# Moving group moments, similarity scaling and a skip connection from VectorE to ScalarE and TensorE in a 16-image Mamba block

## What is computed

```
x = x + L0(gn(x))       # nearest dictionary word of each pixel by cosine similarity;
                        # where (1 - sim)/2 < 0.625 the pixel becomes that word (256 words)
x = x + L1(gn(x))       # layer norm over channels; 4 chunks of 64 channels, each through a Mamba
                        # block (in_proj, causal conv, silu, selective scan with 16 states,
                        # gate by silu(z), out_proj), + skip_scale * chunk; layer norm; proj
```

## Time and profile before

| | |
|---|---|
| time, three runs | 4572.13, 4575.1, 4581.95 us (median 4575.1) |
| span of the profiled execution, its own time as far as it is recorded | 4583.2 us |
| busy share of the span | VectorE 92%, TensorE 83%, GpSimd 75%, ScalarE 56% |
| granted TensorE clock, mean | 0.921 of full speed |
| first multiply of the first image | 147 us after the start |

### The profile page before, as it was taken

One profiled execution on the slowest core, in us unless ns is written; L12 is line 12 of the kernel. 1 busy time (PEld: TensorE's weight loads), 2 busy tenths in 40 slices (PEclk: granted clock), 3 DMA queues, 4 the chain that ended last, 5 costly groups with the idle time before them and its releaser, 6 DMA issues. The chain is left out here.

```text
span 4583.2 us, 51269 instructions
## 1 busy us (share of the span) xinstructions
PE 3800.3 (83%) x13584; PEld 1249.4 (27%) x13584; DVE 4234.4 (92%) x3519; ACT 2572.6 (56%) x3144; POOL 3430.4 (75%) x2085
## 2 busy tenths in 40 slices
PE   3787888888788887988888888888888878888886
PEld 2222323223232222322223232222322223232221
DVE  2699998999999999999999999999999999999997
ACT  2465565655556565565655656555565655656553
POOL 2577777777778787787777877777787777878775
...
GB/s 45 142 158 189 142 197 151 178 184 143 179 148 188 180 154 181 150 183 169 174 179 145 192 146 184 187 138 192 136 186 172 162 181 145 188 160 176 189 160 115
DMA packets 217783, 752.46 MB, mean 164 GB/s; under 512 B 27400, under 2 KB 28816, under 8 KB 213392
## 3 DMA queue, kind: packets, MB, share of 16 engines
...
## 5 line engine op out<-in xcount | busy, mean ns | idle before, releaser
L590 POOL TENSOR_TENSOR state<-state,c_all 128x1024 f32<-128x1024 f32 x1024 | 2399.3, 2359 | 368.8 <-DVE state L960 348.8
L960 DVE TENSOR_TENSOR_SCAN state<-dtb,ub 128x1024 f32<-128x1024 f32 x1024 | 2341.0, 2286 | 51.6 <-ACT dtb L764 5.9
L1184 PE MATMUL ub<-u,spr 64*128 64x512 f32 x4096 | 1313.2, 698 | 454.5 <-DVE state L960 428.8
L764 ACT ACTIVATE dtb<-dtb,a_neg 128x1024 f32<-128x1024 f32 x1024 | 1154.5, 1141 | 537.3 <-DMA dtb<-dt_scratch 480.2
L951 DVE TENSOR_TENSOR ub<-ub,b_all 128x1024 f32<-128x1024 f32 x1024 | 1242.0, 1213 | 63.0 <-issue 30.3
L1184 PEld LDWEIGHTS ub<-u,spr 64*128 64x128 f32 x4096 | 357.4, 199 | 1288.7 <-DVE state L960 887.8
L1200 PE MATMUL yp<-state,gat 128*32 128x512 f32 x4096 | 607.3, 668 | 6.1 <-POOL state L590 6.1
L1053 PE MATMUL mb<-xs,wtap 128*128 128x512 f32 x512 | 244.4, 620 | 19.2 <-DMA xs<-xn 10.6
L657 ACT ACTIVATE e_x<-mb,col 128x512 f32<-128x512 f32 x128 | 88.0, 688 | 259.2 <-PE mb L1067 259.2
L665 ACT ACTIVATE dt<-mb 128x512 f32<-128x512 f32 x128 | 76.2, 595 | 279.4 <-PE mb L1084 279.1
L1067 PE MATMUL mb<-xc,wdt 128*128 128x512 f32 x256 | 160.5, 713 | 58.1 <-DVE ym L841 38.7
...
## 6 DMA issues: line engine op xcount, KB each, us to landing
dtb<-dt_scratch SPq DMA_DIRECT2D x1024, 512.0 KB, 4.8
xs<-xn SPq DMA_DIRECT2D x128, 256.0 KB, 5.2
...
dt_scratch<-dt SPq DMA_DIRECT2D x128, 128.0 KB, 3.7
```

Source lines behind the costliest of these rows:

```text
L590: pool.tensor_tensor(v, v, c_all[:, c % 2, :], ALU.mult).then_inc(gated, 1)
L764: act.activation(dtb[:, k, :], dtb[:, k, :], ACT.Exp, scale=a_neg[:, GROUP[g]:GROUP[g] + 1]).then_inc(decayed, 1)
L960: dve.tensor_tensor_scan(state[:, g % STATES, :], dtb[:, k, :], ub[:, g % 2, :], 0.0, ALU.mult, ALU.add).then_inc(scanned, 1)
L1184: last = pe.matmul(ub[:, g % 2, h * HALF:(h + 1) * HALF], spr[lo:lo + TURN, GROUP[g] % 8, :], u[lo:lo + TURN, c % 2, h * HALF:(h + 1) * HA ...
```

## The change

The three kinds of work leave VectorE:

- `a_stat` and `a_gs` become `a_sum` on ScalarE: for each half one pass that sums x/1024 and one that sums (x/32)^2, both with an accumulator output, the full outputs going to gt as scratch. For g=1 this waits, half by half, for the first layer's result.
- `post_skip` becomes a second matmul by a scaled identity, `skp`, into the same 64 rows of the bank, and `post_take` on ScalarE, which copies the bank to ym and frees it. It stands at steps 14, 17, 14 and 14 of chunks 0 to 3 where the skip stood at 13, 17, 12 with 14, and 12.
- The scaling in `a_pick` becomes `a_near` on ScalarE, into four buffers (sq, both halves of rs and a new one), with sq reused: the ScalarE square for the c-side layer norm waits for the first search. ScalarE frees the bank. `a_pick` and `a_idx` become one, two of them at (0, 31) and two at (1, 1).
- Steps of `a_rstd`, `a_mom`, `a_newton` and `a_hot` are moved to later ones.

```diff
-ACT_BATCH = {(0, 10): ["a_gs00", "a_gs01", "a_rstd0"], (0, 20): ["a_affine00"], (0, 22): ["a_affine01"],
-             (0, 28): ["a_rn", "c_sq0", "c_sq1"], (1, 2): ["c_msq0"], (1, 7): ["c_rs0", "c_msq1"], (1, 8): ["a_oht0"],
-             (1, 12): ["a_oht1"], (1, 13): ["c_rs1"], (1, 25): ["a_gs10"], (1, 26): ["a_gs11"], (1, 27): ["a_rstd1"],
+ACT_BATCH = {(0, 9): ["a_sum00"], (0, 10): ["a_sum01"], (0, 13): ["a_rstd0"], (0, 14): ["post_take0", "post_take1"],
+             (0, 20): ["a_affine00"], (0, 22): ["a_affine01"], (0, 28): ["a_rn", "c_sq0", "c_sq1"],
+             (0, 30): ["a_near0", "a_near1"], (0, 31): ["a_near2", "a_near3"], (1, 2): ["c_msq0"],
+             (1, 7): ["c_rs0", "c_msq1"], (1, 8): ["a_oht0"], (1, 12): ["a_oht1"], (1, 13): ["c_rs1"],
+             (1, 17): ["post_take0", "post_take1"], (1, 24): ["a_sum10"], (1, 25): ["a_sum11"], (1, 28): ["a_rstd1"],
              (1, 30): ["a_affine10", "a_affine11"], (2, 0): ["a_msq0"], (2, 5): ["a_rs0"], (2, 7): ["a_msq1"],
-             (2, 10): ["a_rs1"], (2, 13): ["a_xn0"], (2, 25): ["a_xn1"]}
-DVE_BATCH = {(0, 9): ["a_stat00"], (0, 10): ["a_stat01"], (0, 12): ["a_gm0"], (0, 13): ["post_skip0", "post_skip1"],
-             (0, 31): ["a_pick0", "a_idx0", "a_pick1", "a_idx1", "a_pick2", "a_idx2", "a_pick3", "a_idx3"],
+             (2, 10): ["a_rs1"], (2, 13): ["a_xn0"], (2, 14): ["post_take0", "post_take1"], (2, 25): ["a_xn1"],
+             (3, 14): ["post_take0", "post_take1"]}
+DVE_BATCH = {(0, 12): ["a_gm0"], (0, 31): ["a_pick0", "a_pick1"], (1, 1): ["a_pick2", "a_pick3"],
              (1, 3): ["c_var0", "c_ctr0"], (1, 9): ["c_var1"], (1, 11): ["c_ctr1"], (1, 12): ["a_keep0"],
              (1, 13): ["a_mix00"], (1, 14): ["a_mix01", "a_keep1"], (1, 15): ["a_mix10", "a_mix11"],
-             (1, 17): ["post_skip0", "post_skip1"], (1, 24): ["a_stat10"], (1, 25): ["a_stat11"], (1, 28): ["a_gm1"],
-             (1, 29): ["c_out00", "c_out01"], (1, 31): ["c_out10", "c_out11"], (2, 3): ["a_var0", "a_ctr0"],
-             (2, 9): ["a_var1", "a_ctr1"], (2, 12): ["post_skip0"], (2, 14): ["post_skip1"],
-             (3, 12): ["post_skip0", "post_skip1"]}
-POOL_BATCH = {(0, 10): ["a_mom0"], (0, 13): ["a_newton0"], (0, 23): ["a_xg0"], (0, 28): ["a_xg1"],
-              (0, 31): ["a_hot0", "a_hot1"], (1, 0): ["a_hot2", "a_hot3"], (1, 16): ["c_scale0", "c_scale1"],
-              (1, 18): ["a_x20", "a_x21"], (1, 24): ["a_mom1", "a_newton1"], (2, 0): ["a_scale0"],
+             (1, 28): ["a_gm1"], (1, 29): ["c_out00", "c_out01"], (1, 31): ["c_out10", "c_out11"],
+             (2, 3): ["a_var0", "a_ctr0"], (2, 9): ["a_var1", "a_ctr1"]}
+POOL_BATCH = {(0, 11): ["a_mom0"], (0, 14): ["a_newton0"], (0, 23): ["a_xg0"], (0, 28): ["a_xg1"],
+              (0, 31): ["a_hot0", "a_hot1"], (1, 2): ["a_hot2", "a_hot3"], (1, 16): ["c_scale0", "c_scale1"],
+              (1, 18): ["a_x20", "a_x21"], (1, 26): ["a_mom1"], (1, 28): ["a_newton1"], (2, 0): ["a_scale0"],
               (2, 5): ["a_scale1"]}
...
-        sim = sb("sim", [P, 2, WORDS])
+        sim_last = sb("sim_last", [P, HALF])
...
+        sim = [v.rearrange("p (k w) -> p k w", k=2) for v in (sq[:], rs[:, 0, :], rs[:, 1, :], sim_last[:])]
...
-                    pool.wait_ge(v_pick, 3 * (4 * t + i) + 3)
+                    pool.wait_ge(v_pick, 2 * (4 * t + i) + 2)
...
-                elif name.startswith("a_gs"):
+                elif name.startswith("a_sum"):
                     g, j = int(name[-2]), int(name[-1])
-                    act.wait_ge(v_stat[g], 4 * t + 2 * j + 2)
-                    act.activation(gs[:, 0, j:j + 1], mv[:, j, 0:1], ACT.Copy)
-                    act.activation(gs[:, 1, j:j + 1], mv[:, j, 0:1], ACT.Identity, scale=mv[:, j, 0:1],
-                                   bias=mv[:, j, 1:2]).then_inc(a_gsd[g], 1)
+                    if g == 0:
+                        act.wait_ge(s_x, 16 * (t + 1))
+                        at_least(act, xn_done, NJ * t)
+                    else:
+                        act.wait_ge(x2_done, NJ * t + j + 1)
+                    act.activation(gt[:, j, :], xt[:, j, :], ACT.Identity, scale=1.0 / L,
+                                   accum_out=gs[:, 0, j:j + 1]).then_inc(a_gsd[g], 1)
+                    act.wait_ge(a_gsd[g], 4 * t + 2 * j + 1)
+                    act.activation(gt[:, j, :], xt[:, j, :], ACT.Square, scale=1.0 / 32,
+                                   accum_out=gs[:, 1, j:j + 1]).then_inc(a_gsd[g], 1)
+                elif name.startswith("post_take"):
+                    q = (c - 1) % NC
+                    lo = DM * ((q + h) % 2)
+                    bank, use = banks(kind, b, (f"post_out{h}", c))
+                    act.wait_ge(m_full[bank], use)
+                    if c == 1 and kind != FIRST:
+                        mean_bank, mean_use = banks(kind, b, ("c_mean1", 0))
+                        act.wait_ge(m_free[mean_bank], mean_use)
+                    act.activation(ym[lo:lo + DM, q // 2, cut], mb[lo:lo + DM, bank, :], ACT.Copy).then_inc(m_free[bank], 1)
+                elif name.startswith("a_near"):
+                    i = int(name[-1])
+                    bank, use = banks(kind, b, (f"a_sim{i}0", 0))
+                    act.wait_ge(rn_done, t + 1)
+                    act.wait_ge(m_full[bank], use)
+                    for k in range(2):
+                        last = act.activation(sim[i][:, k, :], mb[:, bank, k * WORDS:(k + 1) * WORDS], ACT.Identity,
+                                              scale=rn[:, 2 * i + k:2 * i + k + 1], bias=minus[:, 0:1])
+                    last.then_inc(m_free[bank], 1)
...
+                    if own == "c":
+                        act.wait_ge(v_pick, 8 * NB if kind in (LAST, "tail") else 8 * (b + 1) + 2)
...
-                elif name.startswith("post_skip"):
-                    h = int(name[-1])
-                    q = (c - 1) % NC
-                    lo = DM * ((q + h) % 2)
-                    bank, use = banks(kind, b, (f"post_out{h}", c))
-                    dve.wait_ge(m_full[bank], use)
-                    if c == 1:
-                        if kind != FIRST:
-                            mean_bank, mean_use = banks(kind, b, ("c_mean1", 0))
-                            dve.wait_ge(m_free[mean_bank], mean_use)
-                    start = PAD + (q + h) % 2 + h * HALF
-                    dve.scalar_tensor_tensor(
-                        out=ym[lo:lo + DM, q // 2, h * HALF:(h + 1) * HALF],
-                        in0=xs[lo:lo + DM, q, start:start + HALF],
-                        scalar=col[lo:lo + DM, C_SKIP:C_SKIP + 1], in1=mb[lo:lo + DM, bank, :],
-                        op0=ALU.mult, op1=ALU.add).then_inc(m_free[bank], 1)
...
-                elif name.startswith("a_stat"):
-                    g, j = int(name[-2]), int(name[-1])
-                    if g == 0:
-                        dve.wait_ge(s_x, 16 * (t + 1))
-                    else:
-                        dve.wait_ge(x2_done, NJ * t + j + 1)
-                    link = chain(v_stat[g], 4 * t + 2 * j)
-                    for h in range(2):
-                        last = dve.bn_stats(stats[:, j, h, :], xt[:, j, h * HALF:(h + 1) * HALF])
-                    link(last)
-                    link(dve.bn_aggr(mv[:, j, :], stats[:, j, :, :]))
...
-                    dve.wait_ge(rn_done, t + 1)
-                    dve.wait_ge(m_full[bank], use)
-                    link = chain(v_pick, 3 * (4 * t + i))
+                    dve.wait_ge(m_free[bank], use)
+                    hold_here(dve)
+                    link = chain(v_pick, 2 * (4 * t + i))
                     for k in range(2):
-                        last = dve.tensor_scalar(sim[:, k, :], mb[:, bank, k * WORDS:(k + 1) * WORDS],
-                                                 rn[:, 2 * i + k:2 * i + k + 1], 1.0, ALU.mult, ALU.subtract)
+                        last = dve.max(best[:, i, k, :], sim[i][:, k, :])
                     link(last)
-                    dve.sem_inc(m_free[bank], 1)
                     for k in range(2):
-                        last = dve.max(best[:, i, k, :], sim[:, k, :])
-                    link(last)
-                elif name.startswith("a_idx"):
-                    i = int(name[-1])
-                    link = chain(v_pick, 3 * (4 * t + i) + 2)
-                    for k in range(2):
-                        last = dve.max_index(where[:, i, k, :], best[:, i, k, :], sim[:, k, :])
+                        last = dve.max_index(where[:, i, k, :], best[:, i, k, :], sim[i][:, k, :])
                     link(last)
...
+            link(dve.tensor_scalar(skp[:], idf[:], col[:, C_SKIP:C_SKIP + 1], None, ALU.mult))
...
-                        lo = DM * ((c - 1 + q) % 2)
+                        last_c = (c - 1) % NC
+                        lo = DM * ((last_c + q) % 2)
+                        first = PAD + (last_c + q) % 2 + q * HALF
                         bank = enter(kind, b, (f"post_out{q}", c))
```

(21 more changed lines are left out.)

7 lines of the change are left out of this document (4 added, 3 removed).

## The result

The changed kernel takes 4510.4 us (median of 4 runs, 4498.73 to 4519.83) against 4576.1 for the kernel before on the same chip: a ratio of 0.9852, 95% interval 0.9828 to 0.9875. That is 66 us gained, where 96 were forecast and 4479 us named. The profiled execution has a span of 4510.2 us.

A forecast was written before the change was run, and what follows sets the result against it. VectorE was taken to set the pace, with TensorE close behind. Six places summed to 6.4 us per turn, times 15 turns 96 us, off the median 4575.1 gives 4479 us; range 4415 to 4541, chance 0.68.

The forecast's parts named there:

- the 280 us: Ceiling of the gain: VectorE's removed work plus its waits on itself, about 280 us, 17.5 per image.
- B: The searches, chunk 0 unit 15 to chunk 1 unit 5: 2.5 us gained per turn, bounds 2.0 and 3.4.
- D: Second moments, chunk 1 unit 10 to chunk 2 unit 1: 2.6 us gained per turn, bounds 1.5 and 3.7.
- A: First statistics and first skip, chunk 0 from unit 4: 1.2 us gained per turn, bounds 0 and 2.4.
- C: Skip of chunk 1, units 8 and 9: 1.3 us lost per turn, bounds 0.85 and 1.7.
- E: Skip of chunk 2, units 6 and 7: 1.3 us gained per turn, bounds 0.8 and 1.5.
- F: Skip of chunk 3, units 6 and 7: 0.1 us gained per turn, bounds -0.3 and 0.5.
- Rival 2: ScalarE's copies free banks late at four places a turn, delaying TensorE: 84 us slower, 4659 us; chance 0.09.
- Rival 1: VectorE keeps nearly all of its removed time, 10.7 to 17.5 us per turn: 4415 to 4313 us; chance 0.17.
- Rival 3: No change, TensorE arriving no sooner and eating the gains up to chunk 2: 4565 to 4585 us; chance 0.06.

The follow-up runs named there:

- run 2: The kernel before with the searches alone changed (ScalarE's scaling passes and the two groups of searches): 4537.7 us, ratio 0.9912.
- run 5: The kernel before with norm matmuls of 64 columns of ones in place of one, nothing else of the change: 4557.1 us, ratio 0.9958.
- run 1: The changed kernel with norm matmuls of 64 columns of ones in place of one: 4451.6 us, ratio 0.9723.
- Run 9: run 1 with first-chunk copies ahead of the root, squares behind four scaling passes, second moments' chain earlier on ScalarE and GpSimd: 4383.3 us.
- run 6: run 1 with ScalarE's two copies of the first chunk's output projection put ahead of the reciprocal root of the first moments: 4435.4 us, ratio 0.9704.
- run 4: The kernel before with the group moments alone changed (ScalarE's summing passes in place of VectorE's statistics, both groups): 4527.5 us, ratio 0.9901.

## Why the forecast was right in its direction and too large

- **The bound and its limits.** Right: VectorE kept the bound and did not keep the 280 us; it stands at 4007.9 us busy with 502 idle, most of it ahead of the multiply (160.0), the first searches (84.1) and the variance (61.9). The forecast named TensorE's spread, rightly, and ScalarE's dt copy, wrongly: the wait of u for it is 39.1 us, no more than the 41 before.
- **B, 2.5 forecast, 0 measured.** The step that failed is the price of TensorE, "2.0 per similarity tile ... and stays ahead by under 1 us". It was read from one turn at 2.4 GHz; in 13 of 14 turns of the changed kernel the tiles run at 1.2. At one clock the sum comes near its number: the part alone gave 2.1 us in B (run 2), and without the fall on either side, runs 5 and 1, the searches to unit 2 gain 24.8 - 22.7 = 2.1 us. Over all of B, to unit 5, it is 41.55 - 39.90 = 1.65 us. The pass was mis-sized, 0.559 us against the 0.40 taken (0.59 was the other bound), and ScalarE's two squares ahead of it were left out: 2.11 us of waiting at full clock, not 1.7. The Trainium skill (ScalarE: Activation LUTs, section What ACT_TABLE_LOAD costs) gives 186 ns + 0.833 ns per element and 93 ns for each operand read from a per-partition column; with two of them that is an estimate of 585 ns for this pass, and the trace agrees: 559 ns, against 398 for the square of 256 columns.
- **D, 2.6 forecast, 1.3 measured.** Taking TensorE's free time as the only limit failed. What came late was a chain: the second moments behind one more state product on GpSimd, ScalarE's normalisation (idle 2.97 us), and the mean matmuls, begun after 2.29 us without a matmul, their first four taking 3.65 us at half clock where the next four take 1.88. With the half clock in 7 of 14 turns, at 1.7 us each, the clock took some 0.8 of the missing 1.3 us here too; what decides in which turns it falls is not shown. The forecast had "moving GpSimd's small steps" at nothing. Run 9 moves them up again together with the root and the order of the normalisation: D gives 2.1 us more, the wait and the half clock are gone, and GpSimd's share of that was not measured alone. The changed kernel, sixth turn:

```profile
1651.85 1.24 ACT L744 ACTIVATE cd<-xt,gsm 128x1024 f32<-128x1024 f32 x1 [2.97 <-POOL gsm L546]
...
1656.62 3.65 PE L1166 MATMUL mb<-gt,mean_w 128*128 128x512 f32 x4 [2.29 <-ACT gt L746]
...
1662.21 0.69 DVE L923 TENSOR_TENSOR rs<-mb,sq 128x512 f32<-128x512 f32 x1 [2.30 <-PE mb L1166]
```

- **A, 1.2 forecast, 1.7 measured.** The arithmetic was right: counted from the multiply of unit 4, the second copy ends 15.84 us later where the skip ended after 17.21 (means of the 14 turns), 1.37 earlier against 1.3 forecast. The holder was another. The reload ends 1.2 us of waits in all (25.8 before), not 2.65 per turn; TensorE's next matmul waits for the copy instead (runs 6 and 9). Where VectorE keeps the skip, moving the moments alone gives 3.3 us (run 4), over the bound of 2.4.
- **C, E, F: -1.3, 1.3 and 0.1 forecast, -0.67, 1.30 and 0.35 measured.** The mis-sized term is the skip matmuls, 1.5 us: the output pair and the skip pair run from 1529.09 to 1531.04, 1.95 us together at full clock, 0.87 more than the pair alone in the earlier trace rows and below the range of 1.08 to 1.89. With 0.87 in its place the forecast's own sums give 0.87 - 0.23 = 0.64 lost in C, as measured, and 1.55 - 0.87 = 0.68 gained in F, of which 0.35 came; F's rest is not explained. The rule of the Trainium skill (TensorE: Matmul & The Clock Gate, section Part 3: Packing small matmuls), as the forecast applied it, gave 1.89 more; the trace does not agree with that use of it.
- **The rivals.** Rival 2's mechanism exists: TensorE waits 51.2 us for the copies, 2.71 in the turn shown. But 35.1 us of it is chunk 0's and 16.1 chunk 2's, two places and not four (run 6 leaves 10.0 and 16.1), and it cost part of a gain. The other rule of the Trainium skill (ScalarE: Activation LUTs, section Rules for kernel authors), as the forecast applied it, would have a copy of 2.2 us; the trace does not agree, it shows 0.587. For the same scaling of 256 columns, though, VectorE took 478 ns and ScalarE takes 559. Rival 1 did not come: idle time rose. Rival 3's numbers did not either.
- **The sum, 6.4 forecast, 4.65 measured per turn.** It fell inside the bounds of 2.3 to 10.7, but B, C and D left their own bounds; A came near its number by another path, and 0.7 us came from units that the forecast does not name. So the fit of the sum is in part luck. Both of the forecast's signs of being wrong came: the skip matmuls cost under 1 us, and the x2 reload does not bind in the changed kernel.
